# The end of the last expert mixture: where chunk 1's roots and rows stand, and who adds up chunk 3's totals

## The reference, cut to what matters

```python
def _L3_ffn_ref(x, ...):
    xn = _layernorm(x, ln_gamma, ln_beta)
    ...
    topk_p, topk_i = jax.lax.top_k(probs, TOP_K)          # two of eight experts
    ...
    for eid in range(N_EXPERTS):
        ...
        out = out + hidden @ down_w[eid].T
    return x + out.reshape(B, S, D)
x = _layernorm(x + _L3_ffn_ref(x, ...), axis=-1)
```

## Time and profile before

| | |
|---|---|
| median of 3 runs | 1140.27 us (1139.15 to 1141.21) |
| profiled execution, its own time | 1142.1 us |
| its span | 1140.4 us |
| mean granted clock of TensorE | 0.93 of full speed |
| busy: TensorE, its weight loads | 990.7 us (87%), 498.5 us (44%) |
| busy: VectorE, ScalarE, GpSimd | 778.5 (68%), 660.7 (58%), 355.0 (31%) |
| the last tile's rows copied | 1121.77 us from the span's start |
| from there to the span's end | 18.6 us |

### The profile page before, as it was taken

How to read it: one execution, slowest core, us unless ns; L and a number is a source line. 1 busy time by engine, 2 the same in 40 slices (tenths; PEclk the granted TensorE clock), 3 DMA queues, 4 the chain that set the end, 5 groups by cost and what they waited for, 6 DMA issues and landing times.

```text
span 1140.4 us, 18920 instructions
## 1 busy us (share of the span) xinstructions
PE 990.7 (87%) x6517; PEld 498.5 (44%) x6517; DVE 778.5 (68%) x1663; ACT 660.7 (58%) x1282; POOL 355.0 (31%) x541
## 2 busy tenths in 40 slices
PE   5599889999988899267999999898899998998992
PEld 2267644544446588232333333386322222224661
DVE  5986677768643211587888887347699888856875
ACT  4765646655554454063777777575377776685451
POOL 7626611101442245411000001121111321645764
PEclk9799989999999899675999999989699999999997
DMA  5930234333530220333333220003234422411332
GB/s 140 171 76 1 86 116 145 128 117 119 166 87 18 69 66 12 90 109 101 101 115 134 71 65 28 1 1 103 98 123 133 139 91 77 109 32 45 98 102 84
DMA packets 98375, 101.70 MB, mean 89 GB/s; under 512 B 13354, under 2 KB 80571, under 8 KB 98199
## 3 DMA queue, kind: packets, MB, share of 16 engines
q1 hardware_dynamic: 86169, 89.28, 26.9%
q0 software_dynamic: 6432, 8.18, 2.5%
q10 hardware_dynamic: 5680, 3.04, 1.0%
HBM read 66.60 MB, written 38.09 MB: 92 GB/s over the span
## 4 chain that ended last, share of the span: by engine, by line
PE 66%; DVE 19%; ACT 4%; issue 4%; POOL 4%; DMA 2%; SPq 0%; DVEq 0%; POOLq 0%; ACTq 0%
PE PS L880 13%; PE PS L896 12%; PE PS L853 8%; DVE negm L1706 6%; PE PS L707 5%; PE PS L702 5%; PE PS L1065 3%; PE PS L1075 3%; PE PS L1195 3%; PE PS L883 2%; PE PS L856 2%; PE PS L904 2%; PE PS L1210 2%; DVE X L1553 1%; ACT arena L1325 1%
## 5 line engine op out<-in xcount | busy, mean ns | idle before, releaser
L1325 ACT ACTIVATE arena<-PS 128x512 f32<-128x512 f32 (+3 forms) x768 | 362.6, 548 | 184.1 <-PE PS L883 117.1
L1706 DVE TENSOR_REDUCE negm<-PS 128x2 f32<-128x1024 f32 (+3 forms) x384 | 404.0, 1087 | 85.0 <-PE PS L853 43.5
L880 PE MATMUL PS<-arena 128*128 128x512 bf16 (+3 forms) x768 | 235.2, 365 | 9.1 <-ACT arena L1325 5.2
L896 PE MATMUL PS<-arena,VPAD 128*32 128x512 f32 (+3 forms) x1536 | 187.4, 559 | 0.1
L853 PE MATMUL PS<-arena 32*128 32x512 bf16 (+3 forms) x768 | 142.8, 373 | 27.1 <-DVE negm L1706 23.3
L853 PEld LDWEIGHTS PS<-arena 32*128 32x128 bf16 x768 | 36.1, 91 | 212.2 <-DVE negm L1706 110.7
L2548 POOL CAST nmp<-negm 128x16 bf16<-128x16 f32 x48 | 12.2, 254 | 357.1 <-DVE negm L1706 239.9
L880 PEld LDWEIGHTS PS<-arena 128*128 128x128 bf16 x768 | 69.8, 98 | 118.6 <-issue 56.3
L702 PE MATMUL PS<-arena,W 128*128 128x512 f32 x144 | 83.2, 712 | 13.0 <-ACT arena L1243 10.6
L707 PEld LDWEIGHTS PS<-W,arena 128*128 128x128 f32 x640 | 79.3, 202 | 14.0 <-issue 7.0
L707 PE MATMUL PS<-W,arena 128*128 128x128 f32 x640 | 81.0, 287 | 2.8 <-DVE arena L1649 2.4
(11 more groups left out here) (335 smaller groups left out, 1534.7 us busy)
## 6 DMA issues: line engine op xcount, KB each, us to landing
arena<-score_q SPq DMA_DIRECT2D x48, 288.0 KB
arena<-score_k SPq DMA_DIRECT2D x48, 288.0 KB
arena<-max_parts SPq DMA_DIRECT2D x48, 256.0 KB
max_parts<-arena SPq DMA_DIRECT2D x36, 256.0 KB, 2.9
score_k<-arena SPq DMA_DIRECT2D x36, 128.0 KB
score_q<-arena SPq DMA_DIRECT2D x12, 384.0 KB
arena<-rows_y SPq DMA_DIRECT2D x16, 256.0 KB, 4.0
arena<-slots SPq DMA_DIRECT2D x46, 65.0 KB, 1.9
```

The costliest lines, as they stand in the source:

```text
L880: mm = pe.matmul(PS[:, b, q0:S], OK[s][:, r, kt * P:(kt + 1) * P], OQ[s][:, r, q0:S], start=True, stop=True)
L896: mm = pe.matmul(PS[32 * r:32 * r + 32, 7, q0:S], VP[:, u, kt, r, :], PB[:, kt % 2, r, q0:S], start=(kt == 0), stop=True, skip_group_check ...
L1325: act.activation(PB[:, kt % 2, r, q0:S], PS[:, 4 + use % 3, q0:S], ACT.Exp, scale=slope(u % G, r) if o["slope"] else 1.0).then_inc(exped, 1)
L1706: vec.tensor_reduce(negm[:, u % 2, 2 * rp:2 * rp + 2, qt], PS[:, 2 * (use % 2):2 * (use % 2) + 2, 0:nk], AX.X, ALU.max, negate=True).then_ ...
```

## The change

Three things are moved or replaced. On GpSimd, chunk 1's roots no longer stand ahead of the return of tile 44 but behind that of tile 45. On VectorE, chunk 1's rows stand after the loop and no longer in beat 49, where they were the last step of the loop. And chunk 3's total 2X + y0 + y1 is made by TensorE, as four products with the identity that add up in bank 6 of PSUM (X, X, y0, y1); VectorE's two additions for chunk 3 are gone, and its statistics and rows of chunk 3 read the total from PSUM. The first two products wait for chunk 3's X and for the counts that stood in this bank, the other two for both of the chunk's loads.

```diff
 END_BEATS = {40: (0, "first"), 41: (0, "tot"), 42: (0, "statistics"), 44: (0, "normalised"),
-             45: (1, "first"), 46: (1, "tot"), 47: (1, "statistics"), 49: (1, "normalised")}
-END_TILES = {39: 0, 44: 1}
+             45: (1, "first"), 46: (1, "tot"), 47: (1, "statistics")}
+END_TILES = {39: 0}
...
+                L = lanes[3]
+                pe.wait_ge(*V.at(3, "o3.ln"))
+                pe.wait_ge(*V.at(WHOLE, "t1.gt"))
+                for n in range(2):
+                    pe.matmul(bank(L.A), ident, L.X, start=(n == 0), stop=False)
+                pe.wait_ge(found3[3], 32)
+                for n in range(2):
+                    mm = pe.matmul(bank(L.A), ident, L.found[:, n], start=False, stop=(n == 1))
+                mm.then_inc(*T.did(3, "e.sum"))
...
                 assert [next(g, None) for g in gates] == [None] * len(GROUP3)
-                left = range(2, B)
-                for c in left:
-                    for step in ("first", "tot", "statistics"):
-                        end_step(c, step)
-                    if c > left.start:
-                        end_step(c - 1, "normalised")
-                end_step(B - 1, "normalised")
+                end_step(1, "normalised")
+                for step in ("first", "tot", "statistics"):
+                    end_step(2, step)
+                summed = chunk_of(lanes[3].A)
+                vec.wait_ge(*T.at(3, "e.sum"))
+                statistics(3, summed, "e")
+                end_step(2, "normalised")
+                normalised(3, summed, lanes[3].X, "e")
...
-                for c in range(2, B):
+                for c in range(1, B):
                     norm(c, "e")
```

More of the change, by code:

```diff
@@ L109 @@
     "o3.tot o3.bn o3.mv r3.lg o3.ln",
-    "e.first e.tot", NORM_V.format("e")])) for late in (False, False, True, True)]
+    "e.first e.tot e.bn e.mv e.ln"])) for late in (False, False, True, True)]
 SCALAR_STEPS = words(" ".join([
@@ L120 @@
     "p1.tr p1.q p1.k p1.v o1.tr o1.out r1.tr r1.lg", numbered("sh.f", 4), "sh.out", EXPERTS_T, "p2.tr p2.q p2.k p2.v",
-    "o2.tr o2.out ch.tr ch.s ch.out p3.tr p3.q p3.k p3.v p3.vs o3.tr o3.out r3.tr r3.lg"]))
+    "o2.tr o2.out ch.tr ch.s ch.out p3.tr p3.q p3.k p3.v p3.vs o3.tr o3.out r3.tr r3.lg e.sum"]))
 PICK = "{0}max {0}eq {0}rank {0}best {0}pick"
@@ L167, with __init__ @@
 class Steps:
-    def __init__(self, sem, engine, chunk_steps, whole_steps, last_only=()):
+    def __init__(self, sem, engine, chunk_steps, whole_steps, last_only=(), all_but_last=()):
         self.sems = [sem(f"{engine}_chunk{c}") for c in range(B)] + [sem(f"{engine}_whole")]
         steps = chunk_steps if isinstance(chunk_steps[0], list) else [chunk_steps] * B
-        self.order = [[name for name in steps[c] if c == B - 1 or name not in last_only] for c in range(B)] + [whole_steps]
+        self.order = [[name for name in steps[c] if name not in (all_but_last if c == B - 1 else last_only)] for c in range(B)] + [whole_steps]
         self.number = [{name: i + 1 for i, name in enumerate(steps)} for steps in self.order]
@@ L208, in sem @@
             return ctx.enter_context(nc.semaphore(name))
-        V = Steps(sem, "vector", VECTOR_STEPS, VECTOR_WHOLE, words("x1.y0 x1.y1 x1.y2"))
+        V = Steps(sem, "vector", VECTOR_STEPS, VECTOR_WHOLE, words("x1.y0 x1.y1 x1.y2"), words("e.first e.tot"))
         A = Steps(sem, "scalar", SCALAR_STEPS, SCALAR_WHOLE)
         PO = Steps(sem, "gpsimd", GPSIMD_STEPS, GPSIMD_WHOLE)
-        T = Steps(sem, "tensor", TENSOR_STEPS, TENSOR_WHOLE, words("o1.tr o1.out r1.tr r1.lg x1.o0 x1.o1 x1.o2 o3.tr o3.out r3.tr r3.lg"))
+        T = Steps(sem, "tensor", TENSOR_STEPS, TENSOR_WHOLE, words("o1.tr o1.out r1.tr r1.lg x1.o0 x1.o1 x1.o2 o3.tr o3.out r3.tr r3.lg e.sum"))
         vec, act, pool, pe, sp = nc.vector, nc.scalar, nc.gpsimd, nc.tensor, nc.sync
```

## The result

| | before | after |
|---|---|---|
| median, 20 runs of each | 1140.99 us (1136.71 to 1144.45) | 1144.58 us (1140.28 to 1147.65) |
| ratio to before, 95% interval | | 1.0032 (1.0021 to 1.0044) |
| profiled execution, its own time | 1142.1 | 1144.4 |
| its span | 1140.4 | 1142.7 |
| start of the last tile's copy | 1121.48 | 1120.97 |

The changed kernel is slower by 0.32%, 3.6 us; the interval reaches from 2.4 to 5.0 us. The forecast was slower by 0.22%, 1142.8 us, with a range up to 1144.1: the direction held, and the measured median lies 0.5 us above the range.

What follows compares the result with a forecast made beforehand. The end was taken as one serial chain: transfers from the last return, then VectorE. Waiting for TensorE's total added 2.50 us, PSUM rows 0.1, a tenth came off for chunk 1's rows: 1142.8 us, slower by 0.22%, range 1140.7 to 1144.1.

Steps and rivals of the forecast that it cites:

- The earlier return and the lost cover: Last return 1.15 us earlier, but SP stands at chunk 1's store, so the first rows_y load goes 1.03 us later.
- the sixteen waits with the store: On SP, from chunk 1's store to the first rows_y load: passing the waits on returns takes 0.94 us.
- The slow clock: TensorE's second pair of products for chunk 3 runs at clock 0.50 and takes 3.83 us; chunk 3's statistics start 2.50 later.
- The rival of the full clock: TensorE still at 1.00 when chunk 3 lands, pair 1.9 us, total 1141.0, not slower; chance 0.08.
- the loads behind the store: Chunk 1's store data delaying the rows_y loads: nothing added, 0.35 us as upper end; skill-based estimate 0.2.
- chunk 3's rows out of PSUM: VectorE's four row operations reading PSUM instead of SBUF: 0.1 us taken of 0.17; skill-based estimate 0.27.
- The statistics out of PSUM: VectorE's statistics of chunk 3 reading PSUM: no extra cost taken, 0.2 us as upper end.
- the base and its width: Forecast set on 1140.27 us, the median of three runs, with 0.3 to 0.4 us added to the range for their spread.
- the line: 1142.55 us, the time above which a measurement can tell slower (about 0.2%, 2.28 us) from no change.
- the third rival: Store holds the loads back (+0.35 us) or chunk 1's roots are slow (+0.8): 1143.2 to 1143.7; chance 0.24.
- The rival of the cheap waits: SP passes its sixteen waits cheaply, loads go at 1126.7 instead of 1127.25, total 1142.3; chance 0.2.

Runs made afterwards that it cites:

- part 1 alone: Kernel before with only chunk 1's roots and rows moved behind the last return, VectorE still adding up chunk 3: end 0.82 us later, ratio 1.0002.
- part 2 alone: Kernel before with only chunk 3's total moved to TensorE, chunk 1's roots where they stood: end 1.57 us later, ratio 1.0022.
- the repetition: The changed kernel measured once more, beside the kernel before on another chip: end 2.61 us later, ratio 1.0021.
- changed at the full clock: Changed kernel with ten more products of X by the identity ahead of TensorE's first pair: end 1.08 us later than before, ratio 1.0011.
- the unread sum: Kernel before plus TensorE's four products, whose sum nobody reads, VectorE still adding: end 0.02 us earlier, ratio 1.0012.
- the late rows: Kernel before with chunk 1's roots behind the last return, loads before chunk 1's held store, its VectorE rows after chunk 2's landing: end 0.10 us earlier, one run.
- the loads first: Four rows_y loads issued ahead of chunk 1's store: in the changed kernel end 1.52 us later than before, ratio 1.0008; with VectorE adding, 0.69 earlier, 0.9998.
- all costs off: Changed kernel with loads before chunk 1's store, store held, seven more products, separate semaphore for chunk 3's second load: end 1.34 us earlier than before, ratio 0.9988.
- the 48 waits: Already-met waits on SP ahead of chunk 0's store, added to two store-held kernels (VectorE or TensorE adding): ends 0.39 and 1.34 us earlier than before, ratios 1.0000 and 0.9978.

## Why the prediction was right and wrong

**The earlier return and the lost cover: right.** "SP waits for the store's rows when the returns have already landed" is what the trace shows. The return was 1.11 earlier (forecast 1.15), the store left 4.66 after the copy (the forecast's 1126.31 is 4.83), and the sixteen waits with the store took 0.95 (forecast 0.94, from the earlier trace rows). The first load was 0.87 later; forecast +1.03, the difference being chunk 1's rows, 1.11 rather than 1.31 us. The run of part 1 alone shows the same term by itself: first load 0.87 later, end 0.82 later.

**The slow clock: right.** "I take 3.83, the same work in the same state": the pair took 3.78, and VectorE was released 3.82 after TensorE had begun. The rival of the full clock did not occur, and the kernel with ten more products shows what it would have given: 1.99 us.

**The terms of the sum that were too small.** "I add nothing" for the loads behind the store: chunk 3's landing was 0.28 later than the loads' issue explains (1.16 against 0.88, between part 2 alone and the changed kernel), just within the 0.35 kept as the upper end; in the second profile of the changed kernel it was 0.13. By the Trainium skill (DMA: Bandwidth & Descriptors, Queues, rings and completion order) each transfer engine takes descriptors in ring order, the store's ahead of the loads'. Both profiles agree with it in direction, and the prediction's estimate from it, 0.2, was nearer than my nothing; that the store's data is the cause was not tried by itself in this order. "Of these 0.17 I take 0.1" for chunk 3's rows out of PSUM: they took 1.36 instead of 1.12, 0.24. By the Trainium skill (VectorE: DVE Perf Modes, Why PSUM operands drop a tier) an f32 source in PSUM goes at one result per cycle; the prediction's estimate from it was 0.27 in all, and the trace agrees with it. The rows that decided compared means of other instructions, 364 with 407 ns, and should not have: chunk 3's own four had taken 0.28 each from SBUF and took 0.34 from PSUM. The statistics out of PSUM took 0.89 against 0.87; nothing was a fair price for them. Together these terms are 0.4 more and the first load 0.16 less, which leaves the end some 0.2 above the forecast: 2.6 forecast, 2.81 and 2.61 measured at the end of the span.

**The step that failed: the base and its width.** "1142.8" stood on 1140.27, the median of three runs, "with 0.3 to 0.4 beyond for a median whose three runs lay 2 us apart". The median of before was 1140.99 in the 20 runs of the result, 0.7 above it, and 1141.21, 1141.84 and 1141.33 (29 to 35 runs on each of three chips), up to 1.6 above it. Single runs of before lie between 1136.71 and 1144.45 in the first set, so three of them fix a median to a microsecond or so, not to 0.3. Moved up by the 0.7 alone, the range would have ended at 1144.8 and held the measured 1144.58. With 1140.99 as the base the same sum of 2.6 gives 1143.6, and the measured 1144.58 is 1.0 above that; of this, 0.2 is the end's. The remaining 0.8 is more than the profiles show. In the repetition the medians lie 3.35 apart and the ratio says 2.4, with 2.61 at the end, and over all kernels ratio and end differ by 0.2 on average, so it is probably spread alone; no run locates it.

**The chances.** 0.55 for slower by over 0.2% and a forecast nearly on the line were fair for 2.6 to 2.8 us. Of the third rival (store or roots hold the loads back) the first half came true in part, with the 0.28 and 0.13 above; the roots did not, since chunk 1's took 1.38 from the return's end, and chunk 2's 0.19 and 1.01 this time. The rival of the cheap waits did not occur: 0.95 from the store to the first load.

## What to carry to other kernels

Moving work off the path to the last semaphore helps only if the queue behind that semaphore is free: here the transfer queue had a store ahead of the loads, and the store waited for the very work that was moved back. Before handing work to TensorE in a tail, look at how long it will have been idle, and after microseconds of idling as here price the work at the half clock; if it must be there, keep it busy until its input lands. Letting each half wait for its own transfer was tried here only together with the other steps. And compare kernels whose runs spread by several microseconds from a common point in the profile, not by medians of a few runs.

## What the runs showed of the hardware

- **Loads beside other work on VectorE or a code fetch.** From the issue of the first of four 256 KB loads to the landing of chunk 2 it took 3.85 to 3.95 us in the eight kernels of the table in which no packet of the code queue ran in between (before, changed twice, changed at the full clock, parts 1 and 2 alone, the unread sum, the late rows), and 4.46 to 4.91 in the six where one did (all others with the loads first). With the late rows the packet moved behind chunk 2's landing, and chunk 2 was fast again, but chunk 3 was not. In every kernel the packet comes between 0.3 us before and 1.3 us after the end of VectorE's rows of chunk 1; that it is VectorE's code is inferred from that.
- **A code fetch inside the last store.** In the three kernels where a packet of the code queue ran at the tail of the last store's data, it took 2.62 to 2.66 us from the end of the last rows to the span's end, in the other eleven 2.3 to 2.4. The packet's 3.9% of 16 engines in half a microsecond is 0.3 us of one engine.
- **A store behind loads.** With a 256 KB store issued right behind the four loads, TensorE, which waits for the last of them, began 6.71 us after the first one's issue. With the store held back it began on the last half 6.02 after it (all costs off), and SP saw the last load landed 6.04 to 6.08 after it (three kernels without the 48 waits).
- **The clock.** The granted clock fell 2.6 us after the end of TensorE's last pass in the kernel before, and over 3.4 us after it in the changed one (1122.58 to between 1126 and 1127). The same four passes of 128x512 took 3.78 at 0.50 and 1.98 to 1.99 at 1.00.
- **A source in PSUM.** Four f32 TENSOR_SCALARs of 128x128 took 1.08 to 1.12 from SBUF (1.31 for chunk 1's in the three kernels where a return ran on GpSimd beside them) and 1.36 from PSUM, in every kernel; the statistics of the same size 0.87 and 0.89.
